# TensorE's one-group loops in the attention and the fused stage written out as straight code

## Time and profile before

| what | value |
|---|---|
| median of three runs | 1389.29 us |
| span of the profiled execution, first to last instruction | 1387.9 us |
| granted TensorE clock, mean over the span | 0.960 |
| PE busy | 1238.4 us, 23094 matmuls |
| DVE, ACT, POOL busy | 944.3, 980.7, 897.7 us |
| DMA, mean | 82 GB/s, 113.96 MB |
| DMA queue q8 (kind instruction), whole span | 56 packets, 0.92 MB |
| instructions of all engines in the profile | 59975 |

### The profile page before, as it was taken

How to read it: one execution, slowest core, us unless ns; L and a number is a source line. 1 busy time by engine, 2 the same in 40 slices (tenths; PEclk the granted TensorE clock), 3 DMA queues, 4 the chain that set the end, 5 groups by cost and what they waited for, 6 DMA issues and landing times. The chain is left out here.

```text
span 1387.9 us, 59975 instructions
## 1 busy us (share of the span) xinstructions
PE 1238.4 (89%) x23094; PEld 1036.4 (75%) x23094; DVE 944.3 (68%) x2136; ACT 980.7 (71%) x1956; POOL 897.7 (65%) x1432
## 2 busy tenths in 40 slices
PE   4999999989999998958999999925889998898997
PEld 2778888777788887937999999924677776675775
DVE  3788888877887886595555555525999999864331
ACT  1677787777888887346788776614888888875553
POOL 2577777777777665216999998758677777413431
PEclk9999999999999999579999999966999999999999
DMA  4233434332222320151322222322232333112221
GB/s 126 71 111 110 121 107 127 108 94 87 84 83 83 91 69 26 35 156 39 89 84 81 81 84 66 65 73 69 76 88 82 89 89 91 59 47 61 69 68 46
DMA packets 140285, 113.96 MB, mean 82 GB/s; under 512 B 17184, under 2 KB 113952, under 8 KB 140192
## 3 DMA queue, kind: packets, MB, share of 16 engines
q1 hardware_dynamic: 131744, 95.42, 23.5%
q0 software_dynamic: 8448, 17.32, 5.0%
HBM read 78.55 MB, written 34.08 MB: 81 GB/s over the span
## 5 line engine op out<-in xcount | busy, mean ns | idle before, releaser
L912 DVE TENSOR_REDUCE at_mx<-at_ps_s 128x16 f32<-128x1024 f32 x128 | 156.1, 1220 | 90.4 <-PE at_ps_s L599 46.3
L818 ACT ACTIVATE at_pt<-at_ps_t 128x1024 f32<-128x1024 f32 x128 | 130.6, 1020 | 54.7 <-PE at_ps_t L613 54.0
L811 ACT ACTIVATE at_pr<-at_dd 128x1024 f32<-128x1024 f32 x128 | 135.2, 1056 | 34.6 <-DVE at_dd L920 34.5
L2452 DVE COPY ex_wt<-experts 128x1156 f32 x133 | 102.8, 773 | 82.3 <-DVE ex_y L2458 74.0
L2410 ACT ACTIVATE ex_hg<-ex_ps_h,ex_wt 128x128 f32<-128x128 f32 x544 | 155.1, 375 | 1.2 <-PE ex_ps_y L2369 1.2
L2338 POOL DMA_INDIRECT ex_xg<-x,ex_ti x136 | 139.0, 1022 | 23.4 <-issue 21.8
L920 DVE TENSOR_TENSOR at_dd<-at_ps_s,at_mx 128x1024 f32<-128x1024 f32 x128 | 153.7, 1202 | 0.1
L2360 PE MATMUL ex_ps_h<-ex_xt,ex_wt 128*128 128x128 f32 x1088 | 147.1, 278 | 1.0 <-ACT ex_xt L2402 0.8
L1992 POOL DMA_INDIRECT l_yg<-rows,l_sl x128 | 126.1, 985 | 31.9 <-issue 29.5
L613 PE MATMUL at_ps_t<-ident,at_pr 128*128 128x128 f32 x1024 | 139.3, 279 | 6.1 <-issue 4.2
L2369 PE MATMUL ex_ps_y<-ex_wt,ex_hg 128*128 128x128 f32 x1088 | 143.7, 275 | 0.4 <-ACT ex_hg L2410 0.4
(11 more groups left out here) (262 smaller groups left out, 3154.5 us busy)
## 6 DMA issues: line engine op xcount, KB each, us to landing
rows<-ex_y SPq DMA_DIRECT2D x136, 64.0 KB
x<-at_ln_out SPq DMA_DIRECT2D x32, 256.0 KB, 3.2
at_kx<-in_xt SPq DMA_DIRECT2D x16, 256.0 KB, 2.8
at_qx<-in_xt SPq DMA_DIRECT2D x16, 256.0 KB, 2.8
at_vin<-in_xt SPq DMA_DIRECT2D x16, 256.0 KB, 2.9
at_xr<-in_x SPq DMA_DIRECT2D x16, 256.0 KB, 3.0
cx<-in_ctx SPq DMA_DIRECT2D x16, 256.0 KB, 3.2
x1t<-at_xt SPq DMA_DIRECT2D x16, 256.0 KB, 3.3
```

The lines of the kernel that those rows point to most:

```text
L811: act.activation(pr[:, p], dd[:, p], ACT.Exp, scale=SCALE).then_inc(p_ready, 1)
L818: act.activation(pt[:, 2 * h + p], ps_t[:, :, :, :], ACT.Copy).then_inc(pt_ready, 1)
L912: dve.tensor_reduce(mx[:, p], ps_s[:, :, 4 * p:4 * p + 4, :], AX.X, ALU.max).then_inc(mx_ready, 1)
```

## The change

TensorE's two calls of the loop helpers become Python loops over integers, so that each group's step is written out with constant waits. No other engine calls these two helpers. The other engines are untouched, and so is the order of TensorE's matmuls and weight loads. 37 loop passes become 37 written-out groups, beside the 14 that were written out before (8 in the attention stage, 6 in the fused stage, where three more than 16 numbers are visited because the step also finishes and begins neighbouring groups).

```diff
@@ attention_phase, _(pe)
-                over_single(pe, step, nl)
+                for g in range(NG * nl):
+                    step(At(nl, g))
@@ fused_phase, _(pe)
-                over_ones(pe, step, -1, NG - 1, NG + 2)
+                for g in range(-1, NG + 2):
+                    step(At(1, g))
```

## The result

The changed kernel takes 1423.12 us (1418.98 to 1426.27, 5 runs) against 1389.06 us (1386.39 to 1390.85, 5 runs): ratio 1.0241, 95% interval 1.022 to 1.0263, 34 us slower. 1415 us had been forecast, in a range of 1391 to 1437.

The account below looks back on a forecast made before the run. TensorE was taken to bound the attention stage, trading work with VectorE in the fused stage. Stalls 22.5 + 7.4, loop costs -5.2, loop exit -1.5 and clock +3 gave +26 us: 1415 us, range 1391 to 1437.

Parts of the forecast that it names:

- The steps that were named: About 160 q8 packets, issue waits of 1 to 2 us around values in some groups, no L613 wait each pass.
- the sum: Whole kernel: stalls 22.5 + 7.4, loop costs -5.2, loop exit -1.5, clock +3, together +26 us.
- Stalls in layers 0 and 1: Attention stage: code waits of 1.02 us a group, none hidden, over 22 newly fetched groups, +22.5 us.
- the wait of 1.5 us: Exit of layer 0's loop: a wait because nothing was fetched ahead, gone in straight code, -1.5 us.
- The fused stage: Fused stage: 12 groups with code stalls of 1.02 us, 60% counted, +7.4 us, less 1.2 us of loop costs.
- the 40% that I had credited: Fused stage: the part of code stalls taken as hidden, since VectorE and ScalarE catch up; 60% was counted.
- Loop costs: Loops removed: -2.9 us in layer 0, -1.1 in layer 1, -1.2 in the fused stage, together -5.2 us.
- The clock: TensorE's clock falls after some long waits: about three falls of 1.4 us each, +3 us allowed.
- Faster: Rival: long straight code is fetched in time, under 0.05 us a packet, only removals stay; 1381 us, chance 0.08.
- No change: Rival: three quarters of the stalls are hidden, costing 8.7 us against 6.7 removed; 1391 us, chance 0.05.
- Much slower: Rival: every group meets one full stall of 2.07 us and the clock falls; 1455 us, chance 0.07.

Follow-up runs that it names:

- the fused half alone: Kernel before with only TensorE's fused-stage loop written out straight; the attention stage keeps its loops: 1396.62 us, ratio 1.0052.
- e10_shifted: Changed kernel with 32 extra narrow products (128 instructions, half a packet) ahead of the attention stage: 1423.51 us, ratio 1.0249.
- The loops with the branch elsewhere: Kernel before, loops kept, second run of values moved from a pass's end to the head of the next: 1385.7 us, ratio 0.9972.
- the split runs: Kernel before with the attention stage's runs of values cut in two by other work: with loops 1444.67 us, with that stage straight 1447.59 us.
- The probe: Kernel before plus narrow products ahead of the fused stage: straight, 128 matmuls every 3.73 us; in a loop, 2.1 us per 128.

## Why the prediction was right

**The mechanism.** The steps that were named happened: packets (about 160 forecast, 167 counted), waits in L627, L632, L1582, L1587 or right behind, several groups with and some without, and the waits at the heads of passes gone. Three groups of layer 0 have neither a wait nor a fall of the clock and take 15.96 us each, where 16.0 was forecast. In size the sum was short, +26 us against +34, and nearly all that is missing lies in the attention stage, forecast at +20 us with the clock and measured at 28.7.

**Stalls in layers 0 and 1.** 1.02 us a group had been taken from the straight stretches. Layer 0 shows 12.8 us of waits in 12 groups, 1.07 each, over 41 packets, 0.31 each against 0.33 forecast. Layer 1 was sized too small: its groups 18 to 29 take 203.9 us against 188.18, 15.7 more where 10.1 followed from the sum (11 x 1.02 - 1.1). Its waits for issue are 14.7 us, 1.2 a group, and one fall of the clock adds 1.7: the term was mis-sized by a fifth, from a sample of 36 packets, and how late a packet begins varies. One reading was wrong: the wait of 1.5 us that was credited as the price of leaving layer 0's loop ends 9 us after the loop's last branch, at an instruction number that leaves 193 with the passes counted once, so it is a wait at a packet's end like the rest.

**The fused stage.** +6.2 us had been forecast (7.4 less 1.2), of which the stage itself took 1.6, or 2.0 in the fused half alone. TensorE's waits in the values products of this stage, changed kernel, then before:

```profile
PE l_ps_o L1582 <- issue: 5.7, 4, 2.0
PE l_ps_o L1587 <- issue: 1.7, 2, 0.9
...
PE l_ps_o L1586 <- issue: 2.0, 2, 1.8
```

They grew by 5.4 us, where 12.2 had been forecast, and 3.2 us of other waits for issue (L1621, L1567) went. So the term was too high mainly because fewer stalls came, and not because VectorE hid more than the 40% that I had credited; why fewer came isn't shown. But that half costs 7.6 us by its median. In its profiled run what follows the stage adds 3.4 us, where the clock fell, a place that the prediction didn't name; where the rest lies isn't shown. Nor is this cost fixed: in e10_shifted, with the same straight code, the fused stage and what follows took 0.4 us more than before.

**Loop costs.** -5.2 us had been credited. The loops with the branch elsewhere gained 4.7 us without any straight code (0.14 to 0.42% of 1390, 1.9 to 5.8 us): the same size. In its profile the attention stage is 3.8 us shorter (498.2 against 502.0 us), where 4.0 had been credited, but the fused stage isn't (269.2 against 267.2), where 1.2 had been.

**The clock.** +3 us had been set aside, three falls of 1.4 us. Three came in the attention stage, 1.7 us each, and one more at the head of the final stage with 3.0 us: some 8 us.

**The rivals.** "Faster" needed under 0.05 us a packet and has 0.31. "No change" nearly holds for the fused stage by itself, where few stalls came, and for the split runs, where TensorE isn't the bound. "Much slower" needed one full wait in each group; layer 0 has seven in 12.

Open: why some packets begin late. The probe's come every 3.4 to 4.0 us; after a run of values of 1.8 us that would make waits of up to 2.2 us, and the changed kernel has some of 2.5. Whether data traffic delays them wasn't tried: of the 12 packets up to 585 us that began more than 2.5 us after the one before was entered, 11 had data on the DMA engines in between, but one had none, and others began early amid traffic.

## What to carry to other kernels

Before writing a loop out, look whether the engine's code queue is silent inside the loop: if it is, nothing has to be fetched there, while straight code has to be delivered at the pace of the fastest run in it. Where that run uses up a packet sooner than the next one comes, here 256 instructions in 1.8 us against 3.7, the engine stands, and the kernel gets longer where that engine is the bound. Ask the same of a loop that is made longer: the pass that lay in 7 packets stayed, those in 8 were fetched again after each branch back. A loop's own cost can be hidden instead: let the branch follow slow instructions.

## What the runs showed of the hardware

- Code of TensorE came in packets of 16 KB, 256 instructions each, one every 3.4 to 4.0 us in the probe, while 256 instructions of narrow fp32 products take 1.8 to 2.1 us.
- Up to 585 us, each wait for code of over 0.25 us ended 1.2 to 1.6 us after a packet had landed; the transfer took 0.9 to 1.6 us, and it began 0.2 to 4.6 us after the packet before was entered.
- A loop pass of 1735 instructions that lay in 7 packets stayed on the engine; passes of 1671 and 1660 that lay in 8 didn't, and each branch back then cost 4.4 us on average in the fused stage and 6 to 7 us, in two waits, in layer 1.
- Of 16 waits for code of over 1 us in the attention stage three were followed within 2 us by 3.4 us at 1.2 GHz, as at 88 us; they took 2.0 to 2.5 us, and another of 2.0 us was followed by none.
